# Zero products in the two 16-head attentions: behind the scores of the first phase and behind the steps of the last

## The reference

```python
q = proj(Wq, bq); k = proj(Wk, bk); v = proj(Wv, bv)      # 16 heads of 8
qb = q.reshape(B, H, nb, bs, hd)                          # bs = 128, nb = 8
scores = einsum('bhnqd,bhnkd->bhnqk', qb, k_ctx) * scale  # own block and both neighbours
mask = (abs(rel) <= 128) & valid
weights = softmax(where(mask, scores, -inf), axis=-1)
out = einsum('bhnqk,bhnkd->bhnqd', weights, v_ctx) @ Wo.T + bo
```

## Time and profile before

| | |
|---|---|
| median of three runs | 3286.94 us |
| profiled execution, its own time | 3289.86 us |
| its span, first to last instruction | 3288.1 us |
| TensorE matmul busy | 2822.4 us (86%) |
| VectorE busy | 1848.9 us (56%) |
| ScalarE busy | 1366.0 us (42%) |
| mean granted TensorE clock | 0.922 of full |

### The profile page before, as it was taken

The page is one execution under the profiler, slowest core; times in us unless marked ns, Lnnn a source line. Parts: engine busy times, 40 slices in busy tenths (PEclk is TensorE's granted clock), DMA queues, the critical chain, the costliest instruction groups (busy, mean ns, idle before and its releaser), DMA issues. The chain is left out here.

```text
span 3288.1 us, 54460 instructions
## 1 busy us (share of the span) xinstructions
PE 2822.4 (86%) x21112; PEld 1419.8 (43%) x21112; DVE 1848.9 (56%) x3584; ACT 1366.0 (42%) x2665; POOL 765.5 (23%) x725
## 2 busy tenths in 40 slices
PE   6667788999988888899678888998889898889988
PEld 3454465333466433344322222342233444565546
DVE  4425553798763688311598888212594544537633
ACT  3314244422243376632367677422204232234552
POOL 1000063365354200000653230002550001230003
PEclk9779599899999899999789999998899998898989
DMA  3031011122012311000312100000430001031102
GB/s 119 16 100 47 13 42 48 60 70 67 11 49 87 76 30 27 2 0 0 66 26 34 24 12 1 1 0 15 112 103 0 1 1 52 21 101 36 33 2 78
DMA packets 84392, 130.03 MB, mean 40 GB/s; under 512 B 15584, under 2 KB 52928, under 8 KB 82856
## 3 DMA queue, kind: packets, MB, share of 16 engines
q1 hardware_dynamic: 71528, 106.68, 12.1%
q0 software_dynamic: 9152, 16.71, 2.1%
q10 hardware_dynamic: 3456, 3.15, 0.3%
HBM read 99.93 MB, written 25.85 MB: 38 GB/s over the span
## 5 line engine op out<-in xcount | busy, mean ns | idle before, releaser
L1811 DVE TENSOR_REDUCE at_mp<-PS 128x1 f32<-128x384 f32 (+3 forms) x640 | 307.0, 535 | 94.6 <-PE PS L1632 82.7
L1760 ACT ACTIVATE at_pt<-PS 128x384 f32<-128x384 f32 (+3 forms) x704 | 272.5, 455 | 198.0 <-PE PS L1632 163.7
L1624 PE MATMUL PS<-at_kx,at_qx 48*128 48x384 bf16 (+5 forms) x640 | 203.1, 354 | 37.2 <-DVE at_mp L1811 21.6
L113 PE MATMUL PS<-zeros 128*128 128x512 bf16 x834 | 208.6, 396 | 1.2 <-DVE mx_y L982 1.2
L1652 PE MATMUL PS<-at_qx,at_kx 57*128 57x512 bf16 (+5 forms) x704 | 196.5, 320 | 9.8 <-ACT at_pt L1760 9.4
L4335 ACT ACTIVATE ls_pt<-PS,ls_far 128x512 f32<-128x512 f32 x256 | 155.4, 684 | 22.5 <-PE PS L4156 18.1
L1632 PE MATMUL PS<-at_above,identb 64*128 64x128 bf16 (+1 forms) x1408 | 164.4, 216 | 0.0
L4482 DVE CUSTOM_DVE_ANT_0 PS<-PS,ls_pt 128x1024 f32<-128x1024 f32 x128 | 153.7, 1239 | 18.1 <-ACT ls_pt L4335 15.5
L1632 PE MATMUL PS<-at_other,at_eye 64*128 64x128 bf16 (+1 forms) x1408 | 162.2, 213 | 0.0
L2540 DVE TENSOR_TENSOR_SCAN mb_ring<-PS,mb_ring 128x1024 f32<-128x1024 f32 x64 | 146.6, 2290 | 18.9 <-POOL mb_ring L2473 6.7
L1133 DVE SCALAR_TENSOR_TENSOR X<-PS,small_L,X 128x512 f32<-128x512 f32 x8 | 6.0, 750 | 261.2 <-PE PS L1080 261.2
(11 more groups left out here) (839 smaller groups left out, 6330.6 us busy)
## 6 DMA issues: line engine op xcount, KB each, us to landing
rw_arena<-rw_v_rows SPq DMA_DIRECT2D x32, 512.0 KB, 4.7
dl_arena<-in_fir_bank SPq DMA_DIRECT2D x32, 256.0 KB, 3.2
lnA<-mb_rows SPq DMA_DIRECT2D x16, 512.0 KB, 3.7
XN<-mb_rows SPq DMA_DIRECT2D x16, 512.0 KB, 3.7
ffn_place<-in_ffn_L SPq DMA_DIRECT2D x4, 1152.0 KB, 17.0
x_rows<-mx_t SPq DMA_DIRECT2D x16, 256.0 KB, 2.5
mx_s<-y_rows SPq DMA_DIRECT2D x16, 256.0 KB, 5.0
ffn_place<-in_ffn_L SPq DMA_DIRECT2D x4, 1024.0 KB, 8.0
```

Of the source, the lines that this page charges most:

```text
L113: k.nc.tensor.matmul(k.PS[:, bank, :], k.zeros16[:, 0:P], k.zeros16[:, :], start=start, stop=start, skip_group_check=True)
L1624: mm = nc.tensor.matmul(PS[:, n % 3, 0:e - c], QX[rows, u % 3, g, blk(i, P)], KX[rows, u % 3, g, c:e], start=True, stop=True)
L1760: nc.scalar.activation(PT[:, y % SLOTS, g, 0:e - c], PS[:, 3 + n % 3, 0:e - c], ACT.Exp, scale=SCALE).then_inc(exp_done, 1)
L1811: nc.vector.tensor_reduce(best, sc, AX.X, ALU.max).then_inc(s_maxed, 1)
```

## The change

Three edits in TensorE's program of `head_attention`. Line 1505 issues 88 zero products instead of 68 (60 instead of 44 in the windowed attention). In phase 0, one zero product into bank 6 follows each score with its masks. In phase 8, from step 2 to the last, two zero products into bank 0 follow the values, behind a wait for the last maximum of all units.

```diff
                     pe.wait_ge(rest_done, 3)
-                    keep_pe_busy(k, 2, 68 if causal else 44)
+                    keep_pe_busy(k, 2, 88 if causal else 60)
...
                             for n in asked:
                                 score_masks(p, n // HG, n % HG)
+                            if p == 0 and asked:
+                                keep_pe_busy(k, 6, 1)
                             if 1 <= p <= UNITS and x < G2:
                                 turned_masks(p - 1, x, t)
                         if 1 <= p <= UNITS and 1 <= x <= G2:
                             values(p - 1, x - 1)
+                        if p == UNITS and 2 <= x < G2:
+                            pe.wait_ge(s_maxed, N1 * UNITS)
+                            keep_pe_busy(k, 0, 2)
                     if 1 <= p <= UNITS and G2 == NX:
                         values(p - 1, G2 - 1)
```

## The result

The kernel after is slower: in four runs of each in the same session 3329.9 us (3306.72 to 3337.49) against 3282.7 (3273.81 to 3288.47), a ratio of 1.013 with a 95% interval of 1.0097 to 1.0163. The forecast was slower, but by 20 us; 3329.9 us lies above its range of 3289 to 3315. One more execution of the kernel after, in the run after_again, took 3739.5 us at a mean granted clock of 0.718, far slower than any other, and is left out of every ratio.

What follows compares the result with a forecast made beforehand. VectorE was taken to bound causal phase 0, TensorE and VectorE nearly sharing the windowed one, a TensorE-ScalarE round trip phases 8. 7.0 + 5.9 + 9.6 - 1.8 - 0.1 = +20.6 us gave 3307 us on the median, range 3289 to 3315.

Steps and rivals of the forecast that it cites:

- What bounds the kernel, and that TensorE becomes the bound in phase 0: Phase 0: TensorE replaces VectorE as bound in the causal attention, 31.0 us (+7.0); windowed 23.8 us (+5.9).
- the 7 that I gave as a sign: Causal phase 0 in the profile after: VectorE idle some 7 us, waiting for TensorE.
- What a zero product costs: On TensorE: 0.216 us in a row, but about 0.10 us more at each change of how the array is cut.
- the rival of hidden change-overs: Phases 0 and 8: weight loads are pulled ahead, so products cost only +6.3 us, 3293 us in all; chance 0.14.
- so I take phases 0 and the start of phase 1 at full clock: Ahead of phase 0: more products cost 0, shrink the idle stretch to some 1.3 us and give full clock.
- third rival: Phases 0 stay at half clock: causal about 54 us, windowed about 40, total 3348 us; chance 0.05.
- What the clock gives back in phases 1: Phases 1 at full clock from the start: windowed -1.8 us, causal -0.1 us.
- Edit 3: Phase 8: 18 pairs of zero products stand on the loop, 0.54 us each, +9.6 us in all.
- The clock there was 1.00 already: Phase 8: clock already full before the change, so its added products bring no time back.
- The second rival: Windowed phases 3 to 7: four half-clock stretches of 2.62 us each vanish, 3297 us with all gone; chance 0.16.

Runs made afterwards that it cites:

- after_again: The kernel after, unchanged, run once more; ratio 1.0126 (1.0089 to 1.0162) to the kernel before, from three executions.
- no_gap: Kernel before plus one zero product behind each phase 0 score, and 100 and 72 products ahead of the first score; ratio 1.0048 (1.0023 to 1.0072).
- phase0_only: Kernel before plus only one zero product behind each score of phase 0, products ahead left at 68 and 44; ratio 1.0137 (1.0094 to 1.0179).
- after_no_gap: Kernel after with 100 and 72 zero products ahead of the first score instead of 88 and 60; ratio 1.0088 (1.0060 to 1.0116) to before.
- phase8_only: Kernel before plus only the two zero products behind steps of phase 8; ratio 1.0009 (0.9989 to 1.0029).
- two_behind: Kernel before plus 88 and 60 products ahead and two zero products behind each phase 0 score; ratio 1.0107 (1.0037 to 1.0177).
- half_rows_closed: Kernel before plus 64-row zero products behind phase 0 scores (but the last four), and 94 and 66 whole products ahead; ratio 0.9988 (0.9969 to 1.0007).
- one_with_data: Kernel before plus 88 and 60 products ahead and one product on non-zero data behind each phase 0 score; 3300.4 us, executed once.
- ahead_only: Kernel before with only the 88 and 60 zero products ahead of the first score; ratio 0.9993 (0.9964 to 1.0023).

## Why the prediction was wrong, step by step

*What bounds the kernel, and that TensorE becomes the bound in phase 0*: right. no_gap shows 31.04 and 24.00 us against the sum's 31.0 and 23.8. VectorE was idle for 4.9 of the 31.0 us, not for the 7 that I gave as a sign.

*What a zero product costs*: right. At full clock no_gap shows 0.32 us from a product to a score (1096.32 to 1096.64) and 0.15 from a mask of 128 columns to a product (1096.74 to 1096.89); the rival of hidden change-overs fell.

*Edit 1, "so I take phases 0 and the start of phase 1 at full clock"*: this step failed, in two ways. First, I took the idle stretch to shrink to 1.3 us, by subtracting from the load of one execution. It was 2.46 us in the causal attention after, and 0.91 to 2.84 us in the seven profiled executions with 88 products, since the landing of the load moves by 2 us between them. Second, I took a shorter stretch to be enough. Behind up to 1.34 us the phase entered at 1.00 and held it for 13.7 us or longer; behind 1.98 us or more it was at 0.50 within 1.9 us and stayed there.

This is the third rival's "phase 0 stays at half clock", to which I gave 0.05; its price of 54 and 40 us was near the 52 and 39 to 40 measured. Its evidence stood in the earlier trace rows: TensorE busy for 22.23 of 23.90 us and still at 0.50. I answered it with a stretch that edit 1 "fills", which it only shortens. My other argument against it, that activity alone releases the clock, was not borne out either: 51.80 us busy of 51.80 stayed at 0.50. Its total of 3348 us was not reached, because the windowed phase 0 after held 1.00 for 13.7 us and windowed phases 2 to 7 came out shorter.

The totals bear this out. Edit 2 behind the long stretches (phase0_only) has a ratio of 1.0137 (1.0094 to 1.0179), with the stretch closed (no_gap) 1.0048 (1.0023 to 1.0072): the intervals don't touch. With all three edits the kernel after is at 1.013 and after_no_gap at 1.0088, where the forecast's 20.6 us make 1.0063; these two intervals overlap.

The size of no_gap, 15.8 us on 3282.8 (7.6 to 23.6 by its interval), is above the forecast's 12.9 for phases 0 less 1.9 given back in phases 1. A part of that is the 32 and 28 more products ahead, which no longer fit behind the load. From the first product to the first score no_gap took 22.3 and 16.25 us; the eleven profiled executions with an idle stretch over 0.6 us took 20.7 and 14.6 in the median (products and stretch added up). That makes the cost some 3 us, an estimate.

In the profile after, causal phase 0 at half clock adds 52.0 - 31.0 = 21.0 us to the sum, the fallen part of the windowed one 31.2 - 24.0 = 7.2, and the fall in causal phase 8 3.0; windowed phases 2 to 7 and the rest of the program take off 7.8 and 3.2.

*What the clock gives back in phases 1*: undersized where it is given. At 1.00 from the start, phases 1 took 28.77 and 22.44 us in no_gap, 1.2 and 3.2 less than before, not 0.1 and 1.8: I took a later phase as measure, which also turns the outputs of the unit before. In the kernel after, phases 1 began at 0.50 and gave 0.7 and 0.8.

*Edit 3*: the mechanism was right and the term a little large, 8.7 us instead of 9.6. By the steps of phase8_only against before, a pair added 0.53 or 0.54 us to eleven of the sixteen steps that can be compared, and 0.23 to 0.39 to the other five; why these hide a part is not shown. "The clock there was 1.00 already" did not hold in every execution: after and after_no_gap had 10.2 us at 0.50 in the causal phase 8, from 3.3 us in it, which made 35.8 us of 32.2. In the profile after this fall, at 1371.5, comes before the first pair of edit 3, at 1374.35. Over all profiles three of eight phases 8 with edit 3 fell, and three of twenty without (in two_behind, phase0_only and half_rows_closed). That edit 3 protects against such falls is not shown anywhere.

*The second rival*, that the windowed stage's four stretches at 0.50 in phases 2 to 7 would go: in part right, -7.8 us in the profile after, which had one. Of the thirteen profiles other than before's, six had none, six had one and no_gap had two. phase8_only, whose windowed stage has the code of before up to phase 8, had one where the profile before had four. So they move from execution to execution, and I count the -7.8 us as luck of the profile before; that the change has no part in it is not shown.

What stays open: why two products raised the clock in the causal phase and not in the windowed one; what lets the windowed phase fall at 13.7 and 15.0 us, behind the turn of the maxima, in two executions and not in no_gap; and why seven of the ten executions of no_gap took some 14 us or more longer, at a lower mean clock, than the one profiled. The profiles tie the clock of phase 0 to the idle stretch ahead of it; that nothing else decides is not shown.

## What to carry to other kernels

Products that are to keep the clock should close the idle stretch at its longest, not at the one of the profile at hand: here causal phase 0 took 31.1 us behind 1.29 us of idle time (one_with_data) and 52.0 behind 2.46 (after), with the same number of products ahead. Closing it has its own price, some 3 us in no_gap by the estimate above.

Before putting idle work between instructions that use part of the array, count its change-overs and the work of the other part that it displaces: here 48 products of 0.216 us cost 7 us at full clock and 28 at half.

Where another engine sets the pace, as VectorE did with 24.0 us in the causal phase 0, a low clock costs next to nothing, and there is little to win by raising it. No variant here is shown to beat the kernel before: ahead_only and half_rows_closed, whose phases 0 were no longer than before's, come out the same in total.

## What the hardware showed that was not expected

The clock depended on more than what was being streamed. The same instructions of windowed phase 0 with two products behind each score ran 30.72 us at 1.00 when entered at 1.00 and 53.19 us at 0.50 when entered at 0.50; with one product behind each, the causal phase ran 31.04 or 52.05. And a TensorE without a gap can stay at 0.50: 51.80 busy of 51.80 us in causal phase 0 after. Zeros and data showed no difference, by one run with data: behind 0.55 us of idle time (zeros) and 1.29 us (data) both held 1.00 through the causal phase.
